# Second cross attention of a perceiver block: six of thirteen context chunks arrive turned by transfer, the next LayerNorm is made inside it, and the query and key weights are split in pieces

## The reference

```python
a = jnp.einsum('bqd,bkd->bqk', query, key)      # query = LayerNorm(x), key = context
e = jax.nn.softmax(a, axis=-1)
c = jnp.einsum('bqk,bkd->bqd', e, key)          # x = x + c
...
xq = (x @ wq.T).reshape(B, T, n_heads, hd)      # here x = LayerNorm(x + c)
xk = (x @ wk.T).reshape(B, T, n_heads, hd)
xv = (x @ wv.T).reshape(B, T, n_heads, hd)
xq, xk = rotary_pos_emb(xq), rotary_pos_emb(xk)
```

## Time and profile before

| | us |
|---|---|
| median of 3 runs | 2758.86 (2756.78 to 2764.29) |
| profiled execution, device time | 2761.41 |
| its span, first to last instruction | 2759.6 |
| PE busy in the span | 2585.0 (94%) |
| first transposes of the changed stage | at 2380.68 |
| last residual of the stage | at 2539.80 |
| first product of the self attention | at 2557.11 |
| last product of its query, key and value part | at 2601.52 |

### The profile page before, as it was taken

How to read it: one execution, slowest core, us unless ns; L and a number is a source line. 1 busy time by engine, 2 the same in 40 slices (tenths; PEclk the granted TensorE clock), 3 DMA queues, 4 the chain that set the end, 5 groups by cost and what they waited for, 6 DMA issues and landing times. The chain is left out here.

```text
span 2759.6 us, 42889 instructions
## 1 busy us (share of the span) xinstructions
PE 2585.0 (94%) x17220; PEld 2320.8 (84%) x17220; DVE 1769.6 (64%) x1991; ACT 1445.4 (52%) x2585; POOL 1318.9 (48%) x939
## 2 busy tenths in 40 slices
PE   7999999999999999999999999997986988898768
PEld 6899999999999999999999999997874555543547
DVE  3266776667766677677666776666455999633463
ACT  3365566556655566556655665555435443322472
POOL 2344655564574385465556457433004995000262
PEclk9999999999999999999999999999996999899869
DMA  5410110011011111011001101001613000550100
GB/s 193 153 48 24 53 58 24 26 53 63 24 55 48 39 48 55 24 53 58 24 26 53 63 24 55 24 26 40 214 65 136 0 1 16 195 191 32 66 1 16
DMA packets 89883, 163.23 MB, mean 59 GB/s; under 512 B 7715, under 2 KB 57123, under 8 KB 87131
## 3 DMA queue, kind: packets, MB, share of 16 engines
q1 hardware_dynamic: 81370, 152.17, 16.4%
q10 hardware_dynamic: 8320, 8.39, 0.9%
HBM read 142.64 MB, written 17.89 MB: 58 GB/s over the span
## 5 line engine op out<-in xcount | busy, mean ns | idle before, releaser
L357 POOL TENSOR_TENSOR xa_pt_lo<-xa_st,xa_pt_hi 128x1024 fp32r<-128x1024 f32 x255 | 510.6, 2030 | 593.7 <-ACT xa_pt_hi L543 593.7
L54 PE MATMUL xa_kv_ps<-ctx_wv_hi,ctx_hi 128*128 128x256 f32 (+1 forms) x1664 | 467.6, 281 | 3.1 <-DVE xa_v_lo L634 3.1
L56 PE MATMUL xa_kv_ps<-ctx_wv_hi,ctx_lo 128*128 128x256 f32 (+1 forms) x1664 | 469.8, 282 | 0.0
L55 PE MATMUL xa_kv_ps<-ctx_wv_lo,ctx_hi 128*128 128x256 f32 (+1 forms) x1664 | 465.3, 280 | 0.0
L54 PE MATMUL xa_kv_ps<-ctx_hi,ctx_wk_hi 128*128 128x402 f32 (+1 forms) x1024 | 356.2, 348 | 2.7 <-DVEq L711 2.2
L56 PE MATMUL xa_kv_ps<-ctx_hi,ctx_wk_lo 128*128 128x402 f32 (+1 forms) x1024 | 353.2, 345 | 0.0
L55 PE MATMUL xa_kv_ps<-ctx_lo,ctx_wk_hi 128*128 128x402 f32 (+1 forms) x1024 | 352.6, 344 | 0.0
L634 DVE TENSOR_TENSOR xa_v_lo<-xa_kv_ps,xa_v_hi 128x512 fp32r<-128x512 f32 (+1 forms) x224 | 146.3, 653 | 265.7 <-ACT xa_v_hi L516 264.7
L54 PEld LDWEIGHTS xa_kv_ps<-ctx_wv_hi,ctx_hi 128*128 128x128 f32 (+1 forms) x1664 | 306.5, 184 | 3.3 <-DVE xa_v_lo L634 3.3
L55 PEld LDWEIGHTS xa_kv_ps<-ctx_wv_lo,ctx_hi 128*128 128x128 f32 (+1 forms) x1664 | 308.5, 185 | 0.0
L56 PEld LDWEIGHTS xa_kv_ps<-ctx_wv_hi,ctx_lo 128*128 128x128 f32 (+1 forms) x1664 | 306.7, 184 | 0.0
(11 more groups left out here) (388 smaller groups left out, 6299.2 us busy)
## 6 DMA issues: line engine op xcount, KB each, us to landing
n_nat<-in_ctx SPq DMA_DIRECT2D x24, 1024.0 KB, 7.3
ctx_raw<-in_ctx_t SPq DMA_DIRECT2D x24, 804.0 KB, 6.6
ctx_wk_raw<-in_xa_wk SPq DMA_DIRECT2D x64, 256.0 KB, 2.8
ctx_wv_raw<-in_xa_wv SPq DMA_DIRECT2D x32, 512.0 KB, 4.4
q_raw<-in_xa_wq SPq DMA_DIRECT2D x8, 1024.0 KB, 4.7
q_scratch<-q_q_sb ACTq DMA_DIRECT2D x8, 1024.0 KB, 4.4
xa_q_raw<-q_scratch SPq DMA_DIRECT2D x64, 128.0 KB, 2.6
o_scratch<-xa_o_sb SPq DMA_DIRECT2D x64, 128.0 KB, 1.7
```

The costliest lines, as they stand in the source:

```text
L54: nc.tensor.matmul(out, left[0], right[0], start=first, stop=False)
L55: nc.tensor.matmul(out, left[0], right[1], start=False, stop=False)
L56: return nc.tensor.matmul(out, left[1], right[0], start=False, stop=last)
L357: nc.gpsimd.tensor_tensor(by_chunk(pt_lo, p), scored(j, p).rearrange("p g q c -> p g c q"), by_chunk(pt_hi, p).bitcast(F32), ALU.subtract) ...
```

## The change

Three things change together.

**Chunks by transfer.** `TURNED = 7`: chunks 0 to 6 of each batch are turned on PE as before, 14 pairs for a row tile where 26 were. The columns from 896 on (chunks 7 to 12) are loaded from `ctx_t`, an input that holds the context turned and that the first cross attention reads already, by 4 transfers a row tile (310 and 395 columns, each for two batches). They go into the same `turned` buffer, which is single, so they are asked for when all scores of the row tile before are done. The context rows are held in two parts: `front` (chunks 0 to 6, two slots) and `back` (chunks 7 to 12, one slot). So the back rows of r + 1 are asked for only when the values of r have read them. PE waits before the scores of column tile 2 and 3 for the turned columns, and before the values of a group's first chunk for its rows.

**LayerNorm inside.** The block `sa_ln` is gone. A `RowNorm` of row tile r - 1 is made in the loop of row tile r: statistics on DVE after the residual, the root on ACT ahead of the exponentials (with a table load for the root and one for the exponential), the scaling on DVE ahead of the maxima, 4 transposes on PE after the values of chunk 8, the high part on ACT and the low part on DVE ahead of the residual. Row tile 3 has its turn in the self attention block, up to the fifth unit.

**Weights in pieces.** The query and key weights are asked for at the end of the context attention and lie ready. ACT makes the high and DVE the low part of each in 4 pieces of 128x512, PE waits for each piece in the units of row tile 0, and POOL splits nothing. The value weights follow in 4 pieces between units 1 to 4.

The core of the diff:

```diff
-        self.nat = scope.sb("nat", [P, 2, 2, self.NC, H])
+        self.GROUPS = [(0, 4), (4, self.TURNED), (self.TURNED, self.NC - 1), (self.NC - 1, self.NC)]
+        self.front = scope.sb("front", [P, 2, 2, self.TURNED, H])
+        self.back = scope.sb("back", [P, 2, self.NC - self.TURNED, H])
+        self.turned = scope.sb("turned", [P, 2, KC, self.S])
...
+    def load_turned(self, sp, r):
+
+        ends = [self.TURNED * P, self.TILES[2][0] + self.TILES[2][1], self.S]
+        for h in range(2):
             for b in range(2):
+                sp.dma_start(self.turned[:, b, :, ends[h]:ends[h + 1]],
+                             self.ctx_t[2 * r + b][:, :, ends[h]:ends[h + 1]]).then_inc(self.turned_in[h], 16)
...
-        layernorm_transposed(nc, "ca_ln", x_sb, xt, None, ident, lambda sp: context.load_groups(sp, 1, range(NG - 2)))
+        layernorm_transposed(nc, "ca_ln", x_sb, xt, None, ident, lambda sp: context.load_turned(sp, 0))
...
         def _(sp):
-            context.load_groups(sp, 1, range(NG - 2, NG))
-            for r in range(2, RT):
+            for g in range(2):
+                context.load(sp, 1, g)
+            for r in range(RT - 1):
+                sp.wait_ge(s_full, (r + 1) * NT)
+                context.load_turned(sp, r + 1)
                 for g in range(NG):
-                    sp.wait_ge(pv_done, (r - 2) * NG + g + 1)
-                    context.load_groups(sp, r, [g])
+                    to = r + 2 if g < 2 else r + 1
+                    if to < RT:
+                        sp.wait_ge(pv_done, r * NG + g + 1)
+                        context.load(sp, to, g)
+            load_next(sp)
...
+                if t >= 2:
+                    pe.wait_ge(context.turned_in[t - 2], (r + 1) * 32)
...
+                if r > 1 and t == 0:
+                    pe.wait_ge(norm.xt_lo_set, r - 1)
...
+                    if c == GROUPS[context.group_of(c)][0]:
+                        context.wait(pe, r, b, context.group_of(c))
...
                     values(r, c)
-                    for i in ahead[:1 + (c % 2 == 0)]:
+                    if c == TURN_AT and r > 0:
+                        norm.turn(pe, r - 1)
+                    for i in ahead[:1]:
                         transposes(r + 1, i)
...
+                if r > 0:
+                    norm.deviation(act, r - 1)
+                    nc.scalar.activation(norm.root[:, :], norm.eps_sb[:, :], ACT.Exp)
                 exponentials(r)
...
+                if r > 0:
+                    norm.low(dve, r - 1)
                 residual(r)
+                if r + 1 < RT:
+                    norm.statistics(dve, r)
...
-            layernorm_transposed(nc, "sa_ln", x_sb, xt_hi, xt_lo, ident, load, prepare)
...
                 for n, (i, r) in enumerate(units):
-                    pe.wait_ge(w_lo_set, i + 1)
+                    if n == 4:
+                        norm.turn(pe, LAST)
+                    if r == LAST:
+                        pe.wait_ge(norm.xt_lo_set, RT)
...
                     for k in range(KC):
+                        if r == 0:
+                            pe.wait_ge(w_lo_set, i * KC + k + 1)
```

More of the change, by code:

```diff
@@ L914, in turn @@
         for k in range(self.KC):
-            end = self.nc.tensor.transpose(self.t_ps[:, r, k * P:(k + 1) * P], self.xn[:, r, k * P:(k + 1) * P],
-                                           self.ident[:, :])
+            ks = slice(k * P, (k + 1) * P)
+            end = self.nc.tensor.transpose(self.place(r)[:, ks], self.xn[:, r % self.slots, ks], self.ident[:, :])
         end.then_inc(self.turned, 1)
@@ L1861, in group_of, with part, chunk, load @@
         return [g for g, (a, z) in enumerate(self.GROUPS) if a <= c < z][0]
-    def load(self, sp, r, g, b):
+    def part(self, r, b, a, z):
+        n = self.rows(a)
+        if z <= self.TURNED:
+            return self.front[0:n, r % 2, b, a:z, :]
+        return self.back[0:n, b, a - self.TURNED:z - self.TURNED, :]
+    def chunk(self, r, b, c):
+        return self.part(r, b, c, c + 1)[:, 0, :]
+    def load(self, sp, r, g):
         a, z = self.GROUPS[g]
         n = self.rows(a)
[L1866 to L1871, removed]
-            for b in range(2):
-                self.load(sp, r, g, b)
-def context_attention(nc, x_sb, xt, context, ident):
-    S, NC, GROUPS, nat = context.S, context.NC, context.GROUPS, context.nat
+        for b in range(2):
+            sem = self.front_in[r % 2][b][g] if g < 2 else self.back_in[b][g - 2]
+            sp.dma_start(self.part(r, b, a, z),
+                         self.ctx[2 * r + b, a * P:a * P + (z - a) * n].rearrange("(c p) h -> p c h", p=n)).then_inc(sem, 16)
+    def load_turned(self, sp, r):
+        ends = [self.TURNED * P, self.TILES[2][0] + self.TILES[2][1], self.S]
+        for h in range(2):
+            for b in range(2):
+                sp.dma_start(self.turned[:, b, :, ends[h]:ends[h + 1]],
+                             self.ctx_t[2 * r + b][:, :, ends[h]:ends[h + 1]]).then_inc(self.turned_in[h], 16)
+    def wait(self, eng, r, b, g):
+        if g < 2:
+            eng.wait_ge(self.front_in[r % 2][b][g], (r // 2 + 1) * 16)
+        else:
+            eng.wait_ge(self.back_in[b][g - 2], (r + 1) * 16)
+def context_attention(nc, x_sb, xt, context, ident, norm, load_next):
+    S, NC, GROUPS, TILES, turned = context.S, context.NC, context.GROUPS, context.TILES, context.turned
     rows = context.rows
-    H = nat.shape[4]
+    H = x_sb.shape[2]
     KC, R = xt.shape[1:]
@@ L1888, in context_attention @@
     NS = 3
-    CHUNKS = [(c, b) for c in range(NC) for b in range(2)]
+    CHUNKS = [(c, b) for c in range(context.TURNED) for b in range(2)]
     NCH = len(CHUNKS)
```

164 lines of the change are left out of this document (98 added, 66 removed).

## The result

The changed kernel takes 2717.85 us (median of 4 runs, 2717.42 to 2718.84). The kernel before took 2759.42 us on the same chip. The ratio is 0.9839, with a 95% interval of 0.9824 to 0.9853. The forecast was 2719.8 us. The profiled execution of after took 2717.42 us, with a span of 2715.6 us where before's was 2759.6: 44.0 us less. The working promised 39.1.

The account below looks back on a forecast made before the run. PE, busy 94% of the span, was taken as the bound. Terms -5.9 - 18.1 + 1.95 - 15.3 + 0.9 - 2.6 = -39.1 us took the median from 2758.9 to 2719.8 us, range 2715 to 2726.

Parts of the forecast that it names:

- First row tile: Context attention: 12 pairs of transposes between the scores go, 16.81 us becomes 10.9, gain 5.9 us.
- Values of row tiles 0 to 2: Context attention: values take 16.25 us instead of 22.29, gain 6.04 us three times, 18.1 us.
- 12.41 / 13 = 0.95: Values in the context attention: a chunk with nothing behind it takes 0.95 us.
- Last values: Last row tile on PE's timeline: the last values were to take 13.1 us.
- LayerNorm inside at no cost but PE's turn: Row tiles 1 to 3: four transposes on PE cost 1.95 us in all; the rest costs nothing.
- Transfers at no cost: Context attention: 9.45 MB a row tile in 33.0 us at the upper rate of 401 GB/s, no wait.
- lower bound of 264 GB/s: Transfers: rate in a window holding start-up; at it 9.45 MB take 35.8 us, two row tiles lose 2.8 us each.
- Rival (c): Context attention: turned columns move so slowly that transfers set the row tiles' pace, below 180 GB/s, slower than before; chance 0.02.
- Seam: Between context and self attention: block starts 15.3 us earlier, units gain 2.6 us, scopes left at the end cost 0.9 us.
- 0.43 us a scope: At the end: four scopes are left instead of two, 0.43 us each, +0.9 us.
- Rival (d): Seam gives more: unit 0 at full clock and short scope ends, -3 us, 2717 us; chance 0.07.

Follow-up runs that it names:

- The chunks alone: Kernel before with only the transfer of six chunks, keeping the LayerNorm block, POOL's split and whole-pass weights: 2732.84 us, ratio 0.9904.
- the later turn: Changed kernel with the turn of the normalised rows behind chunk 11 of the values instead of chunk 8: 2722.32 us, ratio 0.9866.
- the filled kernel: Changed kernel plus transposes of the identity that nobody reads, in three places where PE stands idle: 2715.56 us, ratio 0.9838.
- the kernel with whole passes: Changed kernel with query and key weights made in one pass each instead of four pieces, value weights still in pieces: 2725.71 us, ratio 0.9858.

## Why the prediction held, step by step

- First row tile: 5.90 us, forecast 5.9.
- Values of row tiles 0 to 2: 15.63, 16.37 and 16.37 us, the last two with the turn; forecast 16.25 and 16.90. Together 1.7 us more gain. This is the mis-sized term. The step "12.41 / 13 = 0.95" took the price of a chunk from the one place where PE had just waited 3.31 us and ran at 0.73 of the clock. At full clock it is 0.86. The chunks alone confirm it, and there even behind the wait, where the low clock fell on the transposes of the probabilities (2.93 us) and the 13 chunks took 11.38 us.
- Last values: 13.6 us, forecast 13.1. The clock was 0.62 there, lower than before's. But the 13 transposes ahead of them took 1.73 us instead of 2.17, so the last row tile as a whole came out as forecast (15.33 us against 2.17 + 13.1 = 15.27), by luck: in the second execution of after the same two took 1.57 + 12.12 us, at full clock.
- LayerNorm inside at no cost but PE's turn: true, and the later turn shows by how much (two chunks of cover are needed, four are there).
- Transfers at no cost: true. My lower bound of 264 GB/s came from 2 us at the start of two transfers, with smaller ones still under way; the next two windows of 2 us there show 341 and 388. The queue gives 364 to 408 when full, and binding began at 12.4 MB a row tile, not at 9.45. Rival (c) needed less than 180 GB/s for all 9.45 MB. Even runs of 256 bytes leave 9.45 MB / 32 us = 295 GB/s over a row tile, and PE still didn't wait, so (c) was far off.
- Seam: block start 1.24 us behind the residual (forecast 1.22), first product 1.42 us later (1.65), and from it to the last value product 40.27 instead of 44.41 us, gain 4.1 (the same working gives 15.02 - 0.04 - (11.98 - 1.65) - 0.4 = 4.25). Two more scopes cost 0.86 us at the end (0.9). The prediction's 0.43 us a scope is not the difference of the two figures that it gives, 1.72 - 1.22 = 0.50; the end measured 2.08 - 1.22, which is 0.43 each. From the last value product to the end of the span only 0.2 us more are seen, so some 0.7 us went elsewhere on that way, unexplained; over all traces this part lasts 157.6 to 159.5 us.
- The remainder: 41.7 us are gained in the stretch, 2.5 ahead of it in the profiled execution. The latter goes with the execution, as the two executions of the filled kernel show.

So the forecast's sum was 1.7 us short in the stretch, and the medians differ from it by 2.0 us. Against the second trace of after it was 3.1 us short; the 1.4 us between the two traces are nearly all clock in the last row tile. The values explain 1.7 us in either, and that the rest comes out at nothing in the first is luck. Rival (d) foresaw a larger gain, but from the seam and at full clock in unit 0; the clock there was 0.66. Its time came nearly true, its mechanism did not.

## What to carry to other kernels

Before a duration is taken from a row, read the granted clock of its window: the only row of a kind may lie behind a wait, and here it was 10% too long for that. The work that was moved from the busy engine to the transfers cost nothing here as long as the bytes of a row tile stayed under what the queue gives when full, and that rate is to be read from a window without a start-up in it. Count also how long the issuing queue needs ahead of a block's end. And trace one kernel twice before a gain of one or two microseconds is ascribed to anything.

## What was not expected of the hardware

- Runs of 256 bytes moved at 187 GB/s at a DMA share of 0.95, rows of 2 KB at 398; and 24 issues held SP for 16.2 us, 0.68 us each.
- Two executions of one kernel came 4.3 us apart ahead of any changed instruction, and the same 14 pairs of transposes took 7.2 us or 9.3 us (at 2381.24 in the kernel with whole passes), with the clock.
- Behind the same wait of 3.3 us the clock of unfilled kernels was 0.61 to 0.68 for 4 us in eight traces and 1.00 in three; after's two executions stand on either side. With filling transposes it was 1.00 in all three, and in unit 0 as well, where no unfilled trace had it.
